# A mixture-of-experts layer on one core: parameters, gathers and token weights in another order

## The reference

```python
xn = rms_w * (x * jax.lax.rsqrt(mean(x * x) + EPS))
gate = xn @ wg_W + wg_b + (genre_embed @ gg_W + gg_b)
topk_w, topk_i = jax.lax.top_k(softmax(gate), 2)
h1 = relu(x @ W1[e] + b1[e])
h2 = relu(h1 @ W2[e] + b2[e])
out = x + sum over the two experts of topk_w * (h2 @ W3[e] + b3[e])
```

## Time and profile before

| | us |
|---|---|
| median of 3 runs | 482.25 |
| lowest and highest run | 480.2, 483.4 |
| the profiled execution | 481.19 |
| its span in the trace | 479.5 |
| PE busy | 431.3 (90%) |
| DVE busy | 306.3 (64%) |
| POOL busy | 302.3 (63%) |
| ACT busy | 289.9 (60%) |

### The profile page before, as it was taken

How to read it: one execution, slowest core, us unless ns; L and a number is a source line. 1 busy time by engine, 2 the same in 40 slices (tenths; PEclk the granted TensorE clock), 3 DMA queues, 4 the chain that set the end, 5 groups by cost and what they waited for, 6 DMA issues and landing times.

```text
span 479.5 us, 13384 instructions
## 1 busy us (share of the span) xinstructions
PE 431.3 (90%) x4296; PEld 385.7 (80%) x4296; DVE 306.3 (64%) x531; ACT 289.9 (60%) x608; POOL 302.3 (63%) x457
## 2 busy tenths in 40 slices
PE   7606889999899999999999999899999999999980
PEld 6406768998689889888888998788899999899870
DVE  4898734776657756856856666555566667775550
ACT  6606529877578768778777764544555556554550
POOL 5720742757777776877877776766656666666451
PEclk9956989999899999999999999999999999999997
DMA  8989692555434544240444331322323433112221
GB/s 289 352 227 377 255 327 82 129 151 135 118 71 131 135 68 122 40 68 24 60 73 115 63 61 22 69 47 46 46 46 51 56 46 47 26 24 40 35 34 19
DMA packets 27179, 49.48 MB, mean 103 GB/s; under 512 B 8267, under 2 KB 21645, under 8 KB 24941
## 3 DMA queue, kind: packets, MB, share of 16 engines
q0 software_dynamic: 13632, 18.00, 22.9%
q1 hardware_dynamic: 9280, 30.45, 18.0%
q10 hardware_dynamic: 4205, 0.17, 0.5%
HBM read 40.08 MB, written 17.83 MB: 121 GB/s over the span
## 4 chain that ended last, share of the span: by engine, by line
PE 37%; POOL 26%; issue 12%; DVE 7%; ACT 5%; POOLq 4%; DMA 2%; DVEq 1%; SPq 0%; ACTq 0%
PE bank L1226 25%; POOL out L611 11%; PE bank L1260 7%; POOL area L579 5%; POOL bound L519 2%; ACT area L756 2%; DMA stage<-in_weights 1%; POOLq L597 1%; DVE area L1025 1%; PE bank L1202 1%; POOL cfrom L574 1%; DVE area L1023 1%; PE bank L1182 1%; ACT area L770 1%; PE bank L1273 1%
## 5 line engine op out<-in xcount | busy, mean ns | idle before, releaser
L1226 PE MATMUL bank<-area,w_hi 128*128 128x256 f16 x1536 | 257.0, 275 | 6.2 <-DVE area L1025 5.8
L1226 PE MATMUL bank<-area,w_lo 128*128 128x256 f16 x768 | 210.8, 274 | 0.0
L770 ACT ACTIVATE area<-bank,cprm 128x256 f32<-128x256 f32 (+1 forms) x264 | 132.3, 556 | 78.2 <-PE bank L1226 62.1
L1226 PEld LDWEIGHTS bank<-area,w_hi 128*128 x1536 | 150.7, 99 | 26.3 <-issue 8.2
L1023 DVE CAST area<-area 128x512 f16<-128x512 f32 (+1 forms) x144 | 66.1, 459 | 137.4 <-ACT area L770 127.1
L611 POOL DMA_INDIRECT out<-area,cto x71 | 119.2, 1679 | 41.9 <-issue 29.3
L1025 DVE TENSOR_TENSOR area<-area 128x512 f16<-128x512 f32 (+1 forms) x144 | 99.0, 688 | 5.0
L579 POOL DMA_INDIRECT area<-x_ext,cfrom x65 | 69.6, 1071 | 37.7 <-POOL cfrom L574 27.9
L1260 PE MATMUL bank<-w_hi,area 128*128 x496 | 86.3, 273 | 0.0
L1226 PEld LDWEIGHTS bank<-area,w_lo 128*128 x768 | 75.8, 99 | 9.3
L780 ACT ACTIVATE area<-area,cw 128x256 f32<-128x256 f32 x71 | 32.3, 500 | 71.0 <-DVE area L1030 52.7
(11 more groups left out here) (199 smaller groups left out, 468.9 us busy)
## 6 DMA issues: line engine op xcount, KB each, us to landing
stage<-in_weights SPq DMA_DIRECT2D x10, 1024.0 KB, 6.0
area<-in_x SPq DMA_DIRECT2D x8, 512.0 KB, 7.5
x_ext<-in_x SPq DMA_DIRECT2D x8, 512.0 KB
out<-in_x SPq DMA_DIRECT2D x8, 512.0 KB, 6.9
w_lo<-in_weights SPq DMA_DIRECT2D x4, 1024.0 KB, 8.3
w_hi<-in_weights SPq DMA_DIRECT2D x2, 1024.0 KB, 9.0
out<-area,cto POOLq DMA_INDIRECT x71, 3.9
area<-x_ext,cfrom POOLq DMA_INDIRECT x65, 3.0
```

The lines of the kernel that those rows point to most:

```text
L770: ins = act.activation(to[:, m * T + u * wide:m * T + (u + 1) * wide], ps_h[layer][b][:, a * T + u * wide:a * T + (u + 1) * wide], ACT.Rel ...
L1226: ins = nc.tensor.matmul(banks[m // 2][:, (m % 2) * T + u * wide:(m % 2) * T + (u + 1) * wide], weight, xp[:, cols], start=(k == 0 and n = ...
```

## The change

- `parameters(0)` goes ahead of the first gather on GpSimd, and the parameters of tiles 0 and 1 are copied right behind each of their gathers.
- The two DMAs that write the weights of tokens go from ScalarE to SP, behind the first expert's loads.
- The first four tiles take rank 0 without reading `etile`; GpSimd and TensorE wait for `s_names` at tile 4 instead of at the start. `experts_of_tiles()` goes behind the low parts on VectorE.
- In every step with `late`, `parameters(late)` goes from behind the gather to behind `add_rows`; rank 1's moves from tile 0 to tile 1.
- Warm-up matmuls stand behind the batches 0 to 2 only.
- Tile 33 also ends by halves.

```diff
+FIRST = -(-LEAST // E)
-LOWS_AT, ..., PARAMETERS_AT = {1: 2, 2: 3}, {}, {}, {0: 2, 1: 3}, {0: 1}
+LOWS_AT, ..., PARAMETERS_AT = {1: 2, 2: 3}, {}, {}, {0: 2, 1: 3}, {1: 1}
...
         def pieces_before(i):
-            return i + pair(i) + (1 if i > LAST - 1 else 0)
+            return i + pair(i) + max(0, i - (LAST - 2))
         def by_halves(i):
-            return paired(i) or i == LAST - 1
+            return paired(i) or i >= LAST - 2
...
                 b3_rows(e)
+                if e == 0:
+                    sp.wait_ge(s_dense, 1)
+                    for h in range(2):
+                        first = h * (N // 2 + 1)
+                        sp.dma_start(x_ext[first:first + N // 2, H:ROW].rearrange("(p j) e -> p j e", j=J),
+                                     je(dense)[h * P // 2:(h + 1) * P // 2]).then_inc(s_ext, 16)
...
             def copy_parameters(i, s):
                 experts = []
+                if i == FIRST:
+                    pool.wait_ge(s_names, 1)
                 for u in range(halves_of(i) if paired(i) else 1):
-                    e = pool.value_load(etile[0:1, bass.ds(name_at(i, u), 1)], min_val=0, max_val=E - 1)
+                    e = 0 if i < FIRST else \
+                        pool.value_load(etile[0:1, bass.ds(name_at(i, u), 1)], min_val=0, max_val=E - 1)
...
-                if late is not None:
-                    link(parameters(late))
                 if i + 2 == PAIRED_AT:
                     pool.wait_ge(s_wsq, 4 * E)
...
                 add_rows(i, s)
+                if late is not None:
+                    link(parameters(late))
+
+            pool.wait_ge(s_whole, 1)
+            pool.wait_ge(s_order, 1)
+            link(parameters(0))
             pool.wait_ge(s_ext, (OUT_PARTS + 4) * 16)
             pool.wait_ge(s_from, 1)
             experts_of = []
             for i in range(RING):
                 gather(i, i, tab_from[:, i * SUB:(i + 1) * SUB])
-                if i == 1:
-                    pool.wait_ge(s_whole, 1)
-                    pool.wait_ge(s_order, 1)
-                    link(parameters(0))
-                    pool.wait_ge(s_names, 1)
-                    for n in range(2):
-                        experts_of.append(copy_parameters(n, n))
+                if i < 2:
+                    experts_of.append(copy_parameters(i, i))
...
             act.activation(ex, cand_ex, ACT.Exp).then_inc(s_exp, 1)
-            act.wait_ge(s_dense, 1)
-            for h in range(2):
-                first = h * (N // 2 + 1)
-                act.dma_start(x_ext[first:first + N // 2, H:ROW].rearrange("(p j) e -> p j e", j=J),
-                              je(dense)[h * P // 2:(h + 1) * P // 2]).then_inc(s_ext, 16)
             squares(0)
...
-            experts_of_tiles()
             low_parts(0)
+            low_parts(1, (0,))
             tables()
-            low_parts(1, (0,))
             x_low(0)
             low_parts(1, (1,))
+            experts_of_tiles()
             split(0, 0)
...
-                if b < BATCHES - 1:
+                if b < SUMS_BEHIND_BATCH:
                     keep_busy(WARM_BATCH, ones16[:, :], bank[6])
...
             def weights_at(i):
+                if i < FIRST:
+                    return [0]
+                if i == FIRST:
+                    pe.wait_ge(s_names, 1)
...
-            pe.wait_ge(s_names, 1)
             layer1(0, weights_at(0))
```

More of the change, by code:

```diff
@@ L80 @@
 BEFORE = [max([p for p in range(q) if PLACE[p] == PLACE[q]], default=None) for q in range(CHUNKS)]
-LOWS_AT, SQUARES_AT, SUMS_AT, HIGHS_AT, PARAMETERS_AT = {1: 2, 2: 3}, {}, {}, {0: 2, 1: 3}, {0: 1}
+LOWS_AT, SQUARES_AT, SUMS_AT, HIGHS_AT, PARAMETERS_AT = {1: 2, 2: 3}, {}, {}, {0: 2, 1: 3}, {1: 1}
 for rank in range(FRONT, E):
```

## The result

| | before | after |
|---|---|---|
| median of 4 runs, us | 482.03 | 500.55 |
| lowest and highest | 480.2, 483.4 | 498.73, 502.12 |
| the profiled execution | 481.19 | 502.12 |
| its span | 479.5 | 500.5 |
| mean granted TensorE clock | 0.961 | 0.941 |

The changed kernel takes 1.0385 times as long as before (95% interval 1.0335 to 1.0436), 18.5 us more. The lines of its code lie some lines lower: the transposes are L1186 (L1182 before), the first ReLU's line is L774 (L770), the gather L587 (L579), the copy of the parameters L599 (L588), the add of rows L622 (L611), the parameters L527 to L544 (L519 to L536), the low parts L829 (L825), the weighing L784 (L780). T(n) is again the start of the transposes of tile n.

A forecast was written before the change was run, and what follows sets the result against it. TensorE was taken as the bound from 65 us to the end. 481.2 + 0.5 (start) + 16.5 (late steps) + 0 (tail) = 498.2; with the median 1.06 above the profiled execution 499.3, forecast 499, range 471 to 507.

The forecast's parts named there:

- main term: Late steps: parameters(late) behind add_rows makes TensorE wait for the gather; 7 x 4.0 less 11.5, +16.5 us.
- the clock: Late steps: TensorE's granted clock falls behind each of seven waits, adding 1.7 us each.
- what goes: Late steps: ScalarE's wait for `cprm` goes, taking off 11.5 of 11.9 us; 0.4 of weight sums stay.
- the waits: Late steps: TensorE waits 2.3 us for the gather in each of seven, between 0.3 and 3.8.
- the start: Up to T(2): parameters(0) ahead of the first gather makes it later; +0.5 us, between -2.9 and +2.5.
- The bound, and where the time would go: TensorE bounds from 65 us; sign: seven waits of 2 us or more for the gather at its transposes.
- I cost it at nothing: Start: token weights' write on SP moves chunk 2's issue to about 43.4, with about 3 us cover; nothing.
- The tail: End: tile 33 by halves lets its adds go a us earlier, nothing ends earlier; 0, between -0.3 and +0.3.
- Waits without the clock: Rival, late steps: gather late by 2.0 us at most and the clock holds; +3.0, 485 us; chance 0.13.
- even exchange: Rival, late steps: the new wait, about 1.6 us, costs what the old one did; 482 us; chance 0.13.
- Faster: Rival: GpSimd's small operations get through beside VectorE, gather's second half by T + 7.8; 470 to 473 us; chance 0.25.
- Late rows: Rival, start: SP's short rows land after GpSimd wants to gather, or hold chunk 3 past 54; 502 us; chance 0.05.

The follow-up runs named there:

- experiment 10: Changed kernel, with the old place of parameters(late) and the old GpSimd and VectorE order at the start: 485.24 us, ratio 1.0050.
- experiment 9: Changed kernel, with the old place of parameters(late) and the write of token weights back on ScalarE's queue: 486.58 us, ratio 1.0079.
- experiments 2: Changed kernel, with parameters(late) put back behind the gather and rank 1's back in tile 0: 485.32 us, ratio 1.0074.
- experiment 8: Changed kernel, with the old place of parameters(late), and VectorE's experts_of_tiles and tables ahead of all low parts: 484.94 us, ratio 1.0052.
- experiment 3: Changed kernel, with the odd chunks' low parts from chunk 3 on replaced by a fill with zeros: 480.60 us, ratio 0.9957.
- experiment 6: Kernel before, with late parameters cut into two parts of seven in successive steps behind the parameters' copy, rank 1 whole: 478.04 us, ratio 0.9897.
- experiments 5: Kernel before, with parameters(late) behind the parameters' copy, ranks 2 to 7 two tiles later, rank 2's ahead of the copy: 480.56 us, ratio 0.9932.
- experiment 1: Kernel before, with only parameters(late) moved behind add_rows and rank 1's to tile 1: 497.15 us, ratio 1.0312.
- experiment 4: Kernel before, with parameters(late) behind the copy of the next parameters and ahead of the wait for the weighing: 481.08 us, ratio 0.9962.

## Why the prediction was right, and where its steps were not

The forecast was 499 us, the measured median 500.55. The mechanism of the main term was right; that the sum came so near is in part luck. In the late steps the clock was set 4.1 us too high and what goes 3.7 us too high, and these two errors cancel; the waits and the start were 1.5 and 1.4 us too low. And the profiled executions lie 21.0 us apart, the medians 18.5.

**The bound, and where the time would go: right.** Seven waits of about 2 us at the transposes, each between a late tile and the gather behind it, in the steps named. By their own numbers, for tile 9, against the trace, all from T(12) on: parameters begin +1.5, measured +1.4; VectorE's pair +3.0, measured +3.0; second half of the gather +10.2, measured +10.8; its landing 3.1, measured 2.8; TensorE's arrival +10.9, measured +11.4; wait 2.3, measured 2.16. The parameters' stretch was 6.6 us against 6.2. I had four operations done before the pair and at most one between its halves; it was two before and one per half. The errors are of opposite sign and small.

**The clock: size off.** I added 1.7 us to every wait because 2.3 was nearer to the 2.11 us with a fall than to the 1.69 without. Four of seven falls came: 3 x 1.72 + 2.65 = 7.8 us against 11.9. The premise that the length of the stretch decides failed: 2.32 had no fall, 2.16 had one.

**The wait at tile 22: size off.** I had all seven alike. Tile 22 waited 4.57 us. GpSimd and TensorE there, changed kernel:

```profile
306.91 1.64 POOL L622 DMA_INDIRECT out<-area,cto  x1 [1.28 <-issue]
308.86 1.62 POOL L622 DMA_INDIRECT out<-area,cto  x1 [0.30 <-issue]
...
318.11 1.43 POOL L587 DMA_INDIRECT area<-x_ext,cfrom  x1 [0.86 <-POOL cfrom L582]
319.85 0.95 POOL L587 DMA_INDIRECT area<-x_ext,cfrom  x1 [0.30 <-issue]
```

```profile
307.87 0.60 PE L1186 MATMUL bank<-ident,area 128*128 128x128 f32 x4
...
323.52 1.11 PE L1186 MATMUL bank<-ident,area 128*128 128x128 f32 x4 [4.57 <-DMA area<-x_ext,cfrom]
```

Against late tile 9, counted from T: the second add starts 0.73 us later, from there the parameters end 0.18 sooner, the table copies and the first half of the gather take 0.60 more, the landing is 0.90 longer (3.67 against 2.77), and TensorE arrives 0.36 sooner, since this step has no weight sums: 2.4 us together, which is 4.57 less 2.16. The earlier trace rows hold the hint: tile 22 was the only one that waited 1.69 us already. Seven waits are so 17.4 us against 7 x 2.3 = 16.1. Why the add and the landing are late in this very step the runs don't say; the DMA engines were no busier than at tile 9 (share 0.31 and 0.37 during the landing).

**What goes: right in sum, wrong in its reason.** I took off 11.5 of the 11.9 us lost before. The weight sums, which stay, are 0.35 us in each of six steps, 2.1 us and not 0.4, and the steps keep another 2.0 us in small remainders. So some 7.8 were removed. The term came out as 17.4 of waits + 0.2 at tile 4 + 7.8 of clock - 7.8 = **17.6** (the trace has 17.7), forecast 16.5. And ScalarE's waits for `cprm`, which I said should be gone, aren't; ScalarE's waits between 60 and 330 us, changed kernel:

```profile
ACT area L774 <- POOL cprm L599: 19.7, 7, 3.9
```

They are longer than in the earlier trace rows. The copy stands behind the gather in GpSimd's queue, and the gather is now late itself. TensorE loses the time at the transposes ahead of the ReLU, so that these waits cost nothing more. As a sign in the trace my sentence would have misled; the waits of the engine that is the bound don't.

**The start: +0.5 forecast, +1.9 measured.** The three halves hold three operations, as said. Counted from SP's first load: the gather begins at 19.7 us, forecast 18.9; TensorE's transposes come 4.1 us behind the start of its second half, forecast 3.75; T(0) is at 25.3, forecast 24.2, and T(2) at 42.8, forecast 41.5. So 0.8 of the 1.4 us are the gather's start, 0.3 the landing and 0.2 what lies behind T(0). The step that was off is the begin of the parameters: 12.6 us behind the load, forecast 11.2, so that three operations and not five were done before VectorE's halves began. The scales were written at 11.8, without the 0.4 us gained that I took off, and the first operation came 0.8 behind them, where I had it follow at once.

"I cost it at nothing", of the rows on SP, stays open. Chunk 2's issue came 8.6 us behind the first load, forecast 9.6, and its own consumer did wait for nothing that shows. But the later loads met the first gather on the DMA engines, which I hadn't asked: experiment 10 shows this collision at 2.2 us of T(0) and none of T(2), experiment 9 against 2 shows 1.5 us at T(0) and 2.6 at T(2), and no median shows it. In the changed kernel the gather is later by itself, and the collision is in part over when it comes. That an earlier gather alone brings little agrees with this: in experiment 8 it began 3.3 us sooner, and tile 0 came 0.2 us sooner.

By the Trainium skill, DMA: Bandwidth & Descriptors, section Queues, rings and completion order, descriptors of one queue are consumed in ring order; the prediction's rival had the short rows queue up behind the 2 MB and hold chunk 2. The trace shows the hold-up one stage sooner: SP spends 6.28 us on issuing them, and chunk 2's issue starts 7.1 us later than the rows'.

**The tail: right.** 0 forecast; from T(35) on 29.6 against 29.7 us.

**The rivals.** Waits without the clock, 485, gave 2.0 us each without falls, but four falls came. An even exchange wanted waits of 1.6 us. Faster wanted the gather at T + 7.8; experiment 3 reached T + 8.7 by leaving work out and was 0.4% faster, so the direction of that rival was right and VectorE's hold was what kept it away, as far as a kernel with less work on VectorE can show it. Late rows: GpSimd's first gather waited for its own parameters (the bracket at 55.24), not for the rows.

## What to carry to other kernels

In a queue that runs near its limit, moving a block of small operations doesn't remove its cost but chooses who waits: ask what stands behind the block in each place, and what the other engines do to it in that place. If every place costs, cut the block into pieces that each fit the slack of a step (experiment 6, -1%); moving it whole gave -0.4 to -0.7% at best. And a load that is issued later isn't free because its consumer has time: ask whose transfer it then meets (experiment 10, 2.2 us at T(0)).

## What the runs showed of the hardware that I had not expected

- **One operation per half.** While VectorE runs scalar_tensor_tensor with two inputs in SBUF (1.24 us a half), GpSimd's operations get in one at each border: 1.10, 1.11, 1.11 us at the start, 1.29, 1.01 at tile 9. The Trainium skill, SBUF — State Buffer, section Who interferes with whom, says that a VectorE instruction with two SBUF inputs contends with a GpSimd instruction that reads SBUF, and that the order of issue decides who blocks. These rows agree with it. The row of the kernel before that I weighed against it, an operation of 2.17 us over both halves, shows that the border isn't always enough. Five of the eight L519 take 2.17 us or more there, and three to five of eight in experiments 2, 8 and 10; the runs don't say why.
- **The issue of an indirect gather is held too:** 1.25 and 0.95 us free, 2.11 and 1.80 beside low parts (experiment 8).
- **A gather's landing is longer beside weight loads:** 2.7 to 3.7 us after its second half began in the late steps of the changed kernel, 4.0 to 8.0 us at the start beside weight loads (experiments 2, 8 and 10), and 5.2 to 5.7 in tiles 2 us behind the issue of 1 MB (experiments 5 and 6). The busy share of the DMA engines alone doesn't set it: it was 0.37 at T(13), with 2.77 us, and 0.31 at T(22), with 3.67.
- **Many short rows hold the issuing queue:** two DMAs of 2,048 pieces take 6.3 us on SP's queue and 5.39 on ScalarE's, and the loads behind them wait that long.
- **The clock and idle stretches of TensorE:** a fall behind 2.22, 2.16, 2.15 and 4.57 us of idle, none behind 2.32, 1.91 and 2.06 (changed kernel); in the kernel of experiment 1 a fall behind 2.31, 2.13, 2.16, 2.16 and 4.69, none behind 1.68 and 2.12. The other kernels widen this: a fall behind 1.89 us at T(22) of experiment 3 and behind 2.04 at T(10) of experiment 9, none behind 2.68 at T(7) of experiment 4. So between 1.9 and 2.7 us the length alone doesn't tell. What a fall costs is steady: 1.6 to 1.7 us, 2.65 behind the two stretches of over 4.5.
